# Two edge walks of a graph network layer: when GpSimd may refill the gather slots

## The reference

```python
def _gat_conv(x, edge_index, W, att_src, att_dst, bias, heads, out_ch, concat):
    n = x.shape[0]
    loops = jnp.arange(n)
    src = jnp.concatenate([edge_index[0], loops])
    dst = jnp.concatenate([edge_index[1], loops])
    h = (x @ W).reshape(n, heads, out_ch)
    a_src = jnp.sum(h * att_src[None], axis=-1)
    a_dst = jnp.sum(h * att_dst[None], axis=-1)
    e = jax.nn.leaky_relu(a_src[src] + a_dst[dst], NEG_SLOPE)
    m = jax.lax.stop_gradient(jax.ops.segment_max(e, dst, num_segments=n))
    p = jnp.exp(e - m[dst])
    denom = jax.ops.segment_sum(p, dst, num_segments=n)
    alpha = p / denom[dst]
    out = jax.ops.segment_sum(h[src] * alpha[..., None], dst, num_segments=n)
    ...
# layer 1: 8 heads of 64 channels, concatenated; elu; layer 2: one head of 256 channels
h = jax.nn.elu(_gat_conv(h, edge_index, W1, att_src1, att_dst1, b1, H1, C1, True))
return _gat_conv(h, edge_index, W2, att_src2, att_dst2, b2, 1, D, False)
```

## Time and profile before

| | |
|---|---|
| median of three runs | 3710.98 us |
| profiled execution, its own time | 3708.69 us |
| its span | 3706.9 us |
| mean granted TensorE clock | 0.841 of full speed |
| first and last start of a gather, first walk | 128.7 and 1537.6 us |
| first and last start of a gather, second walk | 1696.1 and 3120.8 us |

### The profile page before, as it was taken

How to read it: one execution, slowest core, us unless ns; L and a number is a source line. 1 busy time by engine, 2 the same in 40 slices (tenths; PEclk the granted TensorE clock), 3 DMA queues, 4 the chain that set the end, 5 groups by cost and what they waited for, 6 DMA issues and landing times. The chain is left out here.

```text
span 3706.9 us, 57874 instructions
## 1 busy us (share of the span) xinstructions
PE 2639.1 (71%) x11245; PEld 1963.1 (53%) x11246; DVE 2394.2 (65%) x7306; ACT 1181.5 (32%) x4644; POOL 1820.5 (49%) x1892
## 2 busy tenths in 40 slices
PE   8577777777777777794666666556666666599998
PEld 6455555555555555573455444444444434566666
DVE  6778777777777778884555545555655666635445
ACT  5533433333333333341222111122222211342332
POOL 0365666566656656304555556666655564501111
PEclk9799998889999898997777777777776776599999
DMA  5466666666666666413444563633333333422220
GB/s 192 148 188 187 192 188 193 185 185 189 188 188 185 188 190 184 122 52 114 139 138 135 136 177 106 181 106 106 102 95 95 96 108 103 138 75 64 68 89 12
DMA packets 230811, 511.90 MB, mean 138 GB/s; under 512 B 49249, under 2 KB 116044, under 8 KB 230611
## 3 DMA queue, kind: packets, MB, share of 16 engines
q0 software_dynamic: 118128, 361.70, 34.6%
q1 hardware_dynamic: 97958, 134.64, 12.0%
q10 hardware_dynamic: 14524, 13.40, 1.1%
HBM read 463.94 MB, written 49.57 MB: 139 GB/s over the span
## 5 line engine op out<-in xcount | busy, mean ns | idle before, releaser
L1329 POOL DMA_INDIRECT weights<-table,w_idx x880 | 840.7, 955 | 718.9 <-issue 313.4
L815 POOL DMA_INDIRECT w_G<-table,w_idx x880 | 854.8, 971 | 605.5 <-issue 299.2
L927 PE MATMUL PS<-w_G,w_S 128*128 128x260 f32 x3520 | 954.4, 428 | 90.9 <-DVE ACC L1016 57.7
L927 PEld LDWEIGHTS PS<-w_G,w_S 128*128 128x128 f32 x3520 | 724.1, 212 | 253.8 <-issue 99.9
L1515 PE MATMUL PS<-weights 128*128 128x257 f32 x1760 | 618.9, 497 | 119.3 <-issue 55.5
L1515 PEld LDWEIGHTS PS<-weights 128*128 128x128 f32 x1760 | 398.9, 247 | 227.8 <-issue 135.7
L1004 DVE TENSOR_TENSOR w_G<-w_G,PS 128x512 f32<-128x512 f32 x660 | 432.3, 683 | 68.2 <-ACT PS L838 31.2
L1710 DVE TENSOR_TENSOR ACC<-ACC,PS 128x257 f32 x464 | 196.3, 423 | 412.1 <-remote 185.7
L1016 DVE TENSOR_TENSOR ACC<-ACC,PS 128x520 f32 x464 | 321.0, 692 | 211.4 <-PE PS L927 83.7
L851 ACT ACTIVATE w_G<-w_G 128x64 f32<-128x64 f32 x1760 | 443.8, 334 | 0.2
L1351 ACT ACTIVATE w_PW<-w_Z 128x4 f32<-128x4 f32 x220 | 45.2, 205 | 1077.9 <-DVE w_Z L1695 785.3
(11 more groups left out here) (324 smaller groups left out, 3422.4 us busy)
## 6 DMA issues: line engine op xcount, KB each, us to landing
w_DR<-rows SPq DMA_DIRECT2D x146, 384.0 KB
weights<-in_L_ffn_w SPq DMA_DIRECT2D x16, 1024.0 KB, 7.7
w_G<-table,w_idx POOLq DMA_INDIRECT x880
weights<-table,w_idx POOLq DMA_INDIRECT x880
table<-ACC SPq DMA_DIRECT2D x49, 260.0 KB
xbuf<-XR SPq DMA_DIRECT2D x8, 1040.0 KB
XR<-xbuf SPq DMA_DIRECT2D x7, 1040.0 KB, 5.4
table<-row ACTq DMA_DIRECT2D x49, 129.0 KB, 2.2
```

Source lines behind the costliest of these rows:

```text
L815: pool.indirect_dma_start(G[:, r, b, :], None, table, IndexOn(ap=idx[:, r, b:b + 1], axis=0)).then_inc(fetched[r], 16)
L927: last = pe.matmul(PS[:, 2 * at + a, 0:W // layer.banks], lhsT, rhs, start=b == slots[0], stop=b == slots[-1])
L1329: pool.indirect_dma_start(G[:, r, b, :], None, table, IndexOn(ap=idx[:, r, b:b + 1], axis=0)).then_inc(fetched[r], 16)
```

## The change

The wait for `summed` moves into the loop over the slots. It is made before slots 0 and 1 and again before slots 2 and 3, and each time it asks for the same pair of the next batch: the new helper `sums_of_half(b, half)` gives the number of steps that are summed once slots 0 and 1 (half 0) or all slots (half 1) of batch b are done, and b is `before.back(-1)`, the batch behind `before`. So slots 0 and 1 of batch n + 6 wait until slots 0 and 1 of batch n + 1 are summed, and slots 2 and 3 until all of batch n + 1 is. `released` is raised twice per batch. The same edit is made in both walks; the ring keeps its six places, and no other engine's code changes.

```diff
+def sums_of_half(b, half):
+
+    return [k for k, _, slots in steps_of(b) if slots[-1] < 2 * half + 2][-1] + 1
...
             def fetch(n, r, before=None):
                 pool.wait_ge(staged, n + 1)
-                if before is not None:
-                    pool.wait_ge(summed, sums_after(before))
-                pool.sem_inc(released, 1)
                 for b in range(B):
+                    if before is not None and b % 2 == 0:
+                        pool.wait_ge(summed, sums_of_half(before.back(-1), b // 2))
+                    if b % 2 == 0:
+                        pool.sem_inc(released, 1)
                     pool.indirect_dma_start(G[:, r, b, :], None, table, IndexOn(ap=idx[:, r, b:b + 1], axis=0)).then_inc(fetched[r], 16)
```

## The result

The changed kernel takes 3670.52 us in the median of 4 runs (3665.53 to 3678.78), the kernel before 3709.48 us on the same chip (4 runs, 3706.44 to 3718.09). The ratio is 0.9894, with a 95% interval from 0.9873 to 0.9915. The prediction said 3667 us. The profiled execution after has a span of 3671.2 us at a granted clock of 0.84, the same as before (0.841), so the gain is not one of the clock.

The account below looks back on a forecast made before the run. The walks were taken as bound by a cycle of POOL running ahead, everyone slowing, and POOL stopping. The profiled 3708.69 us less 44 for finer stops, with 2.3 added to reach the median, gave 3667 us; range 3590 to 3765 us.

Parts of the forecast that it names:

- No work goes: Both walks: all 1760 gathers stay; the added register instruction and wait per batch count as nothing, at most 132 us of POOL's time.
- The later condition: Refilling the ring in both walks: a place refilled up to one batch later costs 0 us, at most 15 us.
- The finer steps: POOL's gather runs in both walks: stopping after two gathers turns some eights into sixes, gaining 44 us, at most 207.
- The expected signs: In the walks: runs of six and eight, over 118 long waits, idle time before merges down some 40 us together.
- the sum of 44 us: Gain over both walks: 0.1 us a batch times 440 batches, taken off the profiled execution of 3708.69 us.
- My price of 2.2 us for every eight: DVE's loss in a POOL run of eight gathers: 12.39 less two batches of 5.08 us; a six costs 0.95.
- the fifth that I took in the sum: Both walks: of the 0.47 us a batch that sixes could save at most, 0.1 us was taken as an estimate.
- What links runs and stalls: In the walks: long uninterrupted gather runs go with stalls of DVE and PE, short ones don't; the link wasn't visible.
- A: Rival on POOL's rhythm in the walks: the cycle of eight stays, one batch closer; 3711 us, within 10; chance 0.23.
- B: Rival on POOL's stops in the walks: each costs 2.3 us, so more stops are slower; 3754 to 3829 us; chance 0.22.
- C: Rival on gathered rows in the walks: DVE waits because five batches are too few; +15 us, 3726 us; chance 0.05.
- The rule of the Trainium skill: Descriptor writes to SBUF: VectorE can lock GpSimd out, so shorter gather runs free nothing for DVE; sum would be 3711 us.

## Why the prediction was right, and where it was not

*No work goes.* Right: the busy times are the same within 10 us, and the gathers' median is 946 ns both times.

*The later condition.* Right in what it costs. By 1500 us POOL has issued 870 gathers, 217.5 batches, against 215 logits: a lead of 2.5, as worked out. In the second walk up to 2330 us it is 408 gathers, 102 batches, against 100, a lead of 2.0 at that time:
```profile
128.00:1500.00 1372.00, 846.26 (x870) 0.89 0.66 190
```
```profile
128.00:1500.00 1372.00, 75.49 (x215) 0.89 0.66 190
```
```profile
1665.00:2330.00 665.00, 390.31 (x408) 0.78 0.51 142
```
```profile
1665.00:2330.00 665.00, 17.64 (x100) 0.78 0.51 142
```
Counted at every batch from the records, the least lead in the second walk is 1.75 batches before, less than the 2.25 that I had found, and 1.25 after. Even so hardly a row came late, and with the pairs four ahead, with a least lead of 0.5, DVE waits 5.1 us for them there. I had said that no row shows when a gather lands. None of the first chip does; the page of the third has a median of 3.8 us, more than the 2.6 that I took from the experts and still under half of 8.1:
```profile
w_G<-table,w_idx POOLq DMA_INDIRECT x880, 3.8
```
That the later condition gives nothing by itself is measured (ratio 0.999). What I had not said is that it matters together with the steps, by some 25 us: with the pairs six ahead the gain was 0.4%, with the pairs half a batch nearer and four ahead 1.1%. So one sentence of the prediction, that the distance alone leaves the speed as it is, holds, and it has no term for what the two give together.

*The finer steps.* The direction is shown: on the second chip three variants with steps of two, released earlier or later, are all faster than the one with steps of four. The expected signs came: 164 long waits, runs of six, merges that wait 37.1 us less. That the sum of 44 us lies near the 39 measured is luck. The term was put together wrongly in two ways. It was spread over both walks at 0.1 us a batch; measured are 23.4 us in the first walk, 0.11 us a batch, and 7.9 in the second, where the idle time before the merges didn't fall and the variants show no effect of the steps. And it was to come from eights that become sixes. In the first walk 88 eights became 61, with 27 sixes, but most of what went are the deep gaps at the ends of eights: 16 of 88 eights had one before (55.8 us) and 2 of 61 after (6.2 us), while the twelves' 23.7 us came back as the tens' 35.0. My price of 2.2 us for every eight came from a single cycle. At that price the 27 eights fewer alone, as sixes of 0.95, would have brought 34 us in one walk, more than the whole walk gained, while the fifth that I took in the sum was a guess between the bounds. Why the eights that are left mostly end without a deep gap the runs don't show.

*What links runs and stalls.* The prediction took from the rows that long uninterrupted runs go with stalls of the others and that short ones leave them alone. The first half holds in both walks on the first two chips. The second half holds in the first walk only: in the second walk of the kernel before, 11 of the 50 gaps over 3 us (44.1 us) fell at runs of four. As a rule it is wrong: on the third chip 156 gathers in a row slow nobody in the first walk. So the runs don't cause the stalls alone; something that differed between the chips, or between the times at which they ran, and that no row of the trace names, has to be there. My forecast held because the timing was done on a chip of the same kind as the profile.

*The rivals.* A, the kept rhythm, is out on the first chip, since the interval ends at 0.9915 and the mix of runs changed. On the third and fourth chip its time is what came, for a reason that A didn't have: there is no rhythm of running and stopping to break. B, more stops at a loss, is out: the pauses became shorter, 284 us of idle time in 137 of them where it had been 310 us in 116 (counted from the records, first walk), so a stop at every second gather doesn't cost POOL the full 2.3 us each time. C, late rows, is out on the first chip: 0.7 and 17.6 us. On the third chip DVE waits for rows in the second walk already before the change (85.2 us) and a little more after it (89.9 us, one profile each), which is of the size of the 4 us that the change costs there.

*The rule of the Trainium skill* that VectorE locks GpSimd out of its descriptor writes would have given no gain. No run shows such a lock: the gathers take 940 to 949 ns in the minimum and the median on every chip, with DVE 94% busy (1008.62 of 1077 us) on the third as with DVE 78% busy on the first. Whether any of DVE's instructions here works in a two-port mode the trace doesn't say, so the rule itself isn't tested.

What stays open: what makes the stalls on two chips and not on the two others; whether steps finer than two, or coarser than four, move the time on a chip that has them, since those variants met none; why six ahead gives only a third; what the change does in the second walk, if anything; and whether four ahead or half a batch later beats the change (ratios 0.9888 and 0.9893 on another chip, against 0.9894, with intervals that overlap). Taking the gathers away on a chip with stalls, the direct test of the link, wasn't done.

## What to carry to other kernels

When the idle time of a profile comes in bursts, sort the gaps by size and by where they fall in the cycle before pricing the mean cycle: here 16 of 88 runs of eight ended in a gap of over 3 us, and a release of the ring in smaller pieces gave 1% while most of those went. Here a producer that was far ahead did best when let go in small steps, four to five and a half batches ahead of its consumer; the distance alone gave nothing. And a gain that rests on a stall without a known cause should be timed on more than one chip: this one is 1% on one of them and nothing on two others.

## What the runs showed of the hardware

- The same program takes 3709, 3662, 3155 and 3152 us on four chips. The phases beside the walks differ little (873.3 us on the first chip, and 3151.4 - 1157.0 - 1132.6 = 861.8 on the third), the two walks by 544 us.
- On the slower two, DVE is held up late in a run of gathers: in the first walk of the kernel before on the first chip it is busy 0.86 to 0.96 of the time during the first six gathers of a run, 0.76 and 0.43 during the seventh and eighth, and its longest gap is 6.7 us. TensorE stands still there too, and many register instructions take 0.7 us. On the faster two no register or branch instruction takes over 0.4 us, though the gathers are issued in longer runs, take as long (medians of 946 and 948 ns) and move more in the same time (187 and 229 GB/s below).
- The mean granted clock in the stretch from 173 to 1250 us is 0.91 on the first chip and 1.00 on the third. There it goes with engines that stay busy: PE is busy 781 of 1077 us on the first and 860 on the third. These are the rows of both:
```profile
173.00:1250.00 1077.00, 781.08 (x3368) 592.65 (x3369) 835.06 (x2214) 408.35 (x1866) 651.62 (x674) 0.91 0.65 187
```
```profile
173.00:1250.00 1077.00, 860.37 (x4132) 659.13 (x4130) 1008.62 (x2706) 497.85 (x2274) 796.13 (x825) 1.00 0.78 229
```
